# Linear attention between two mixture-of-experts halves on one core: the attention of each sequence in other visits, and later gathers for phase 2

## The reference

```python
x = x + 0.5 * ffn(layernorm(x), W1, b1, W2, b2, Wg, bg)      # first half: "f = 0"
x = x + attn(layernorm(x), Wq, Wk, Wv, proj)
x = x + 0.5 * ffn(layernorm(x), W1, b1, W2, b2, Wg, bg)      # second half: "f = 1"

def ffn(x):    # x is 2 x 2048 x 128; 4 experts, 128 -> 512 -> 128
    idx = argmax(softmax(x @ Wg + bg))                       # one expert per token
    y_e = gelu(x @ W1[e] + b1[e]) @ W2[e] + b2[e]
    return y_e for e = idx
def attn(x):   # linear attention, 32 features
    q', k' = elu(q @ proj) + 1, elu(k @ proj) + 1
    kv = sum over the sequence of k' (outer) v
    return (q' @ kv) / (sum(q') + 1e-8)
```

## Time and profile before

| what | value |
|---|---|
| median of 3 runs | 236.23 us (235.95 to 236.77) |
| the profiled execution's own time | 237.53 us |
| its span, first to last instruction | 235.8 us |
| mean granted clock of TensorE | 0.969 |
| busy: PE, DVE, ACT, POOL | 207.2, 159.4, 126.9, 160.2 us |
| last `finish` on DVE ends | 224.8 us |
| last scatter on POOL ends | 234.2 us |

### The profile page before, as it was taken

How to read it: one execution, slowest core, us unless ns; L and a number is a source line. 1 busy time by engine, 2 the same in 40 slices (tenths; PEclk the granted TensorE clock), 3 DMA queues, 4 the chain that set the end, 5 groups by cost and what they waited for, 6 DMA issues and landing times. The chain is left out here.

```text
span 235.8 us, 6375 instructions
## 1 busy us (share of the span) xinstructions
PE 207.2 (88%) x1786; PEld 195.7 (83%) x1786; DVE 159.4 (68%) x641; ACT 126.9 (54%) x406; POOL 160.2 (68%) x225
## 2 busy tenths in 40 slices
PE   8989996996997999999969998999959899999900
PEld 7879996896997988889969897779959899999900
DVE  3699463579688989698887879788776545553400
ACT  1415055567554586635675676825565567765500
POOL 7221888882728687147138888756878888788775
PEclk9999999998899999999999999999979999999985
DMA  4999259982534462326703852517721976662111
GB/s 103 372 321 254 96 199 351 314 212 83 185 110 167 154 215 69 130 106 237 277 0 116 300 206 83 165 61 281 269 79 42 329 274 222 222 221 103 45 56 45
DMA packets 28454, 41.69 MB, mean 177 GB/s; under 512 B 7795, under 2 KB 14851, under 8 KB 28422
## 3 DMA queue, kind: packets, MB, share of 16 engines
q1 hardware_dynamic: 22368, 34.11, 40.5%
q0 software_dynamic: 3072, 6.82, 11.1%
q10 hardware_dynamic: 2982, 0.36, 1.0%
HBM read 9.41 MB, written 6.82 MB: 69 GB/s over the span
## 5 line engine op out<-in xcount | busy, mean ns | idle before, releaser
L1145 ACT ACTIVATE hT<-U,slab 128x128 f32<-128x128 f32 x304 | 86.7, 370 | 56.4 <-PE U L966 56.3
L966 PE MATMUL U<-hT_in,slab 128*128 (+1 forms) x608 | 82.8, 280 | 1.5 <-ACT hT_in L1139 1.3
L977 PE MATMUL DN<-W,hT 128*128 (+1 forms) x608 | 83.7, 282 | 0.2 <-issue 0.2
L966 PEld LDWEIGHTS U<-hT_in,slab 128*128 128x128 f32 x608 | 74.8, 194 | 2.7 <-issue 2.4
L977 PEld LDWEIGHTS DN<-W,hT 128*128 128x128 f32 x608 | 75.4, 195 | 1.4 <-issue 1.2
L430 POOL DMA_INDIRECT G<-rows,src x64 | 62.5, 977 | 15.2 <-issue 10.2
L729 DVE SCALAR_TENSOR_TENSOR G<-DN,mask,G 128x128 f32 (+1 forms) x76 | 26.4, 348 | 27.3 <-PE DN L977 24.6
L416 POOL MEMSET rest<- 128x512 f32 (+1 forms) x78 | 35.4, 454 | 6.3 <-DVE G L729 0.7
L442 POOL DMA_INDIRECT out_dram<-G x32 | 31.6, 988 | 7.3 <-issue 6.3
L705 DVE TENSOR_SCALAR xn<-G 128x128 f32<-128x128 f32 x64 | 23.7, 389 | 9.3 <-DMA G<-rows,src 9.0
L717 DVE SCALAR_TENSOR_TENSOR G<-slab,mask,G 128x128 f32 (+1 forms) x60 | 21.2, 353 | 6.7 <-DVE G L729 4.0
(11 more groups left out here) (159 smaller groups left out, 219.7 us busy)
## 6 DMA issues: line engine op xcount, KB each, us to landing
slab<-W SPq DMA_DIRECT2D x76, 322.0 KB, 3.1
rows<-G SPq DMA_DIRECT2D x8, 288.0 KB, 2.1
rows<-X SPq DMA_DIRECT2D x4, 512.0 KB, 9.5
X<-in_L_attn_x_dram SPq DMA_DIRECT2D x4, 256.0 KB, 6.7
X<-in_L_attn_x_dram SPq DMA_DIRECT2D x2, 512.0 KB, 8.8
W<-in_L_ffn_W_dram SPq DMA_DIRECT2D x1, 1024.0 KB, 11.5
W<-in_L_ffn_W_dram SPq DMA_DIRECT2D x4, 256.0 KB, 6.0
G<-rows,src POOLq DMA_INDIRECT x64, 3.2
```

Of the source, the lines that this page charges most:

```text
L966: i = eng.matmul(U[s % 3][:, c * P:(c + 1) * P], slab[s % NSLAB][:, c * P:(c + 1) * P], hT_in[ph % 2][:, bass.ds(v * P - expert_at[s], P)] ...
L977: i = eng.matmul(DN[s % 2][:, 0:D], hT[s % NHT][:, c * P:(c + 1) * P], W2[:, bass.ds(expert_at[s] + c * NE * D, D)], start=(c == 0 and not ...
L1145: i = eng.activation(hT[s % NHT][:, c * P:(c + 1) * P], U[s % 3][:, c * P:(c + 1) * P], ACT.Gelu, bias=slab[s % NSLAB][:, F + c:F + c + 1])
```

## The change

It does five things.
1. Attention: group 3's `side_turn` goes ahead of `down` in visit 0, and its `side_kq`, `la_scaled` and exponential follow in the same visit. All four exponentials stand together in visit 0 (one load of a table there, one back in visit 1), where three stood at the end of the phase before and one in visit 1. `la_features` takes groups 0, 1 and then 2, 3. `la_z` is one division over all 16 tiles. `la_fold` moves to visit 2, and the four `lb_num` to visits 3, 4, 4, 5 (before 4, 4, 5, 6), with the `lb_x2` in visits 3, 4, 4, 5.
2. The norms of tiles 8 to 11 stand together in visit 3, those of tiles 12 and 13 (phase 1) or 12 to 15 (phase 2) in visit 5.
3. HOT1 is 6 and no longer 7, and `counts` and `inverse` stand ahead of `up` in their visits and no longer behind it. In phase 2 `inverse` stays in visit 10, where it was.
4. `route_slots` no longer makes the two small tables `end_i` and `flo_i`; `visit_tables` makes them.
5. POOL: the gathers of phase 2 begin in visit LATE1 = 12 (before 11), with ten of them before phase 2 and six in its visits 0 to 2 (before twelve and four). The gathers of phase 3 begin in visit FIRST1 = 10 (before 11). Six scatters stand ahead of them (before seven), and 26 follow (before 25).

The diff, cut to its core:

```diff
-        NORM_MID = (-5, -4, -3, -2, -1, 0, 0, 1, 1, 2, 2, 3, 4, 5, 7, 8)
-        NORM_EARLY = (-5, -4, -3, -2, -1, 0, 0, 1, 1, 2, 2, 3, 4, 5, 6, 6)
+        NORM_MID = (-5, -4, -3, -2, -1, 0, 0, 0, 3, 3, 3, 3, 5, 5, 7, 8)
+        NORM_EARLY = (-5, -4, -3, -2, -1, 0, 0, 0, 3, 3, 3, 3, 5, 5, 5, 5)
-        HOT0, HOT1 = 5, 7
-        FIRST0, FIRST1 = HOT0 + 4, HOT1 + 4
+        HOT0, HOT1 = 5, 6
+        FIRST0, FIRST1, LATE1 = HOT0 + 4, HOT1 + 4, 12
@@ gpsimd
-                if ph > 0 and v == 4:
-                    pow_lb(o, 0)
-                if ph == 2 and v == 4:
-                    scatter(0, 0)
-                if ph > 0 and 4 <= v < 3 + NG:
-                    pow_lb(o, v - 3)
+                if ph > 0 and v in (4, 5, 6):
+                    pow_lb(o, v - 4)
+                if ph > 0 and v == 6:
+                    pow_lb(o, 3)
-            EARLY0, NEXT0, NEXT1 = 8, V - FIRST0, 3 * (V - FIRST1) // 2
-            SCATTERS = {5: (1,), 6: (2,), 7: (3,), 8: (4,), 9: (5,), 10: (6,)}
-            DONE0, PAIRS1 = 7, 10
+            EARLY0, NEXT0, NEXT1 = 8, V - FIRST0, 3 * (V - LATE1) // 2
+            SCATTERS = {v: (v - 4,) for v in range(4, FIRST1)}
+            DONE0, PAIRS1 = FIRST1 - 4, 10
@@ phase 1
-                if v not in (FIRST1, FIRST1 + 1):
-                    attention_pow(1, v)
+                attention_pow(1, v)
-                if v >= FIRST1:
-                    gather_first(1, 0, s, v - FIRST1)
-                if v in (FIRST1, FIRST1 + 1):
-                    attention_pow(1, v)
+                if v >= LATE1:
+                    gather_first(1, 0, s, v - LATE1)
@@ phase 2
-                if v + NEXT1 < T:
-                    gather(1, 0, v + NEXT1)
+                for t in range(NEXT1 + 2 * v, min(NEXT1 + 2 * v + 2, T)):
+                    gather(1, 0, t)
@@ vector, route_slots
-                did(eng.tensor_copy(end_i[:, :], c3[:, 0:NE - 1, T - 1]))
-                did(eng.tensor_scalar(flo_i[:, :], end_i[:, :], 7, None, ALU.arith_shift_right))
@@ vector, by visit (o = ph - 1)
+                if ph in (1, 2) and v == 3:
+                    la_kv(o)
                 finish(s)
                     if v == 1:
-                        la_scaled(o, NG - 1)
+                        la_features(o, 2, NG)
+                        la_z(o, 0, NG)
                     if v == 2:
-                        la_features(o, NG - 1, NG)
-                        la_z(o, NG - 1, NG)
-                    if v == 3:
                         la_gt(o)
-                        la_kv(o)
                     if v == 4:
-                        lb_x2(o, 0)
                         lb_x2(o, 1)
-                    if v in (5, 6):
-                        lb_x2(o, v - 3)
+                        lb_x2(o, 2)
+                    if v == 5:
+                        lb_x2(o, 3)
...
+                if ph in (1, 2) and v == 0:
+                    la_scaled(o, NG - 1)
...
-                        la_features(o, 0, NG - 1)
-                    if v == 1:
-                        la_z(o, 0, NG - 1)
+                        la_features(o, 0, 2)
+                    if v == 3:
+                        lb_x2(o, 0)
@@ tensor, ahead of up
+                if ph < B + 1 and v == hot_at + 2:
                     counts(ph + 1)
+                if ph in (1, 2) and v == hot_at + 4:
+                    inverse(ph + 1, 0, NG)
@@ scalar
-                if late and v == 1:
-                    la_exp(ph - 1, 3, 4)
+                    if v == 0:
+                        la_exp(o, 0, NG)
-                if ph < B and v == 18:
-                    la_exp(ph, 0, 3)
```

More of the change, by code:

```diff
@@ L641, in route_slots @@
                 need(eng, rt["cb"], ph)
-                did(eng.tensor_tensor(wh3[:, :, :], wh[:, :, :], hot[:, :, :], ALU.mult), False)
-                did(eng.tensor_copy(end_i[:, :], c3[:, 0:NE - 1, T - 1]))
-                did(eng.tensor_reduce(pos[:, :], te(wh3), AX.X, ALU.add), False)
-                did(eng.tensor_scalar(flo_i[:, :], end_i[:, :], 7, None, ALU.arith_shift_right))
+                did(eng.tensor_tensor(wh3[:, :, :], wh[:, :, :], hot[:, :, :], ALU.mult))
+                did(eng.tensor_reduce(pos[:, :], te(wh3), AX.X, ALU.add))
                 did(eng.tensor_copy(pos_i[:, :], pos[:, :]))
@@ L661, in visit_tables @@
                 e_no = exp_no[:, 1:NE, 0]
+                ends = cum[:, :].rearrange("p (e t) -> p e t", e=NE)[:, 0:NE - 1, T - 1]
+                did(eng.tensor_copy(end_i[:, :], ends))
+                did(eng.tensor_scalar(flo_i[:, :], end_i[:, :], 7, None, ALU.arith_shift_right))
                 did(eng.scalar_tensor_tensor(out=vis[:, :], in0=flo_i[:, :], scalar=float(T - 1), in1=e_no, op0=ALU.min,
@@ L1018, in la_q @@
             def la_q(b):
-                need(eng, la["z"], 2 * b + 1)
+                need(eng, la["z"], b)
                 for g in range(NG):
@@ L1074, in _ @@
                 ph, v = divmod(s, V)
+                hot_at = HOT0 if ph == 0 else HOT1
+                o = ph - 1
+                if ph in (1, 2) and v == 0:
+                    side_turn(o, NG - 1)
                 down(s)
+                if ph in (1, 2):
+                    if v == 3:
+                        la_kv(o)
+                        la_q(o)
+                    if v == 4:
+                        lb_num(o, 1)
+                    if v == 5:
+                        lb_num(o, 3)
                 for ahead in groups_of(ph, v):
                     turn_in(*ahead)
-                hot_at = HOT0 if ph == 0 else HOT1
                 if ph in (1, 2):
-                    o = ph - 1
                     if v == 0:
-                        side_turn(o, NG - 1)
-                    if v == 1:
                         side_kq(o, NG - 1)
-                    if v == 3:
-                        la_q(o)
-                        la_fold(o)
-                    if v in (4, 5, 6):
-                        lb_num(o, (0, 2, 3)[v - 4])
-                if ph == 0 and v == hot_at + 2:
+                    if v == 2:
+                        la_sum(o, 2, 4)
+                if ph < B + 1 and v == hot_at + 2:
                     counts(ph + 1)
+                if ph in (1, 2) and v == hot_at + 4:
+                    inverse(ph + 1, 0, NG)
                 if ph == 0 and v == hot_at + 4:
@@ L1105, in _ @@
                     if v == 2:
-                        la_sum(o, 2, 4)
-                    if v == 3:
-                        la_kv(o)
-                    if v == 4:
-                        lb_num(o, 1)
-                    if v == hot_at + 2:
-                        counts(ph + 1)
-                    if v == hot_at + (3 if ph == 2 else 4):
-                        inverse(ph + 1, 0, NG)
+                        la_fold(o)
+                    if v in (3, 4):
+                        lb_num(o, 2 * (v - 3))
                 if ph == 0 and v == hot_at + 3:
@@ L1206, in _ @@
                 ph, v = divmod(s, V)
+                if ph in (1, 2) and v == 0:
+                    side_copy((ph - 1) * NG + NG - 1)
                 for ahead in groups_of(ph, v):
```

13 lines of the change are left out of this document (6 added, 7 removed).

## The result

The changed kernel takes 238.22 us (median of 8 runs, 237.07 to 240.03), the kernel before beside it 236.24 us (median of 8, 235.27 to 237.21): ratio 1.0083, 95% interval 1.0054 to 1.0112. It is 2 us slower. The forecast was 234.1 us and faster, with a range up to 237.2. The profiled execution took 238.72 us, with a span of 237.0.

What follows compares the result with a forecast made beforehand. POOL's last unbroken run of gathers and scatters bounds the end, not PE. Its start 3.5 us sooner, less 1.4 for one more scatter, gives -2.1: 235.4 profiled, 1.3 less for the median, 234.1 us; range 232.3 to 237.2.

Steps and rivals of the forecast that it cites:

- The gathers of phase 2: POOL, end of phase 1: first gather issued at 126.0, 2.8 us later than before, behind two powers.
- rival B: DVE, visits 11 and 12 of phase 1: group 1's variance later than about 126, so slower, 236.6 us; chance 0.17.
- signs of being wrong: Final run's start not moving, POOL waiting in it, or group 3's power before 140 or after 144.
- the start of the final run: POOL's phase 3 gathers, then scatters, without waits: start at 172.8, or 3.5 us sooner than 176.05 with phase 0's gain.
- the power of group 3: POOL, phase 2: 9 gathers and one power, 16.1 us after the first gather, so 142.1, no sooner than before.
- the gain of phase 1: Attention and routing of phase 1: counts at 110.5 against 114.27, bounded by 1.0 and 3.8 us earlier.
- PE's wait for the first norm of phase 2: PE, start of phase 2: 2 to 3 us ahead, it waits for the first gather, landing at 129.2.
- rival A: Attention of phase 2: PE's clock falls behind new waits, 1.5 of 3.5 us left, 236.1 us, same time; chance 0.2.
- The tail: POOL, end of the kernel: one more scatter is left for it, costing 1.36 us.
- The slow cast of `end_i`: DVE, `route_slots`: removing it gains 0.15 to 0.55 us per routing; `pos_i` might meet the memset instead.
- Rival C: Group 1's variance sooner or fewer gathers ahead of group 3's power, 1.5 us sooner: 232.6 us; chance 0.13.
- the 0.3 of phase 0: Routing of phase 0: two steps leave `route_slots`, so everything after is 0.3 us earlier, added at the end.

Runs made afterwards that it cites:

- e5: The kernel before, unchanged, run again to have a second profile of it: 236.46 us, ratio 1.0019.
- e6: The changed kernel, unchanged, run again: 238.42 us, ratio 1.0091 to the kernel before.
- e7: Changed kernel with phase 2's gathers begun in visit 11 and group 1's power behind the gathers of visit 12: 234.35 us, ratio 0.9912 to the kernel before.
- e2: Changed kernel with the gather of visit 12 ahead of group 1's power, gathers still from visit 12: 252.91 us, 1.0089, on the chip where all were slow.
- e8: e7 with phase 1's visit tables and masks one visit later, behind group 1's variance: 232.99 us, ratio 0.9847 to the kernel before.
- e12: e8 with seven scatters of phase 2 ahead of phase 3's gathers and 25 behind: 233.61 us, ratio 0.987 to the kernel before.
- e9: Kernel before with only phase 2's gathers begun in visit 12, behind group 1's power, six of them in phase 2: 236.98 us, ratio 1.0037.
- e4: Same kernel as e9, run on the chip where all were slow: 251.82 us, ratio 1.0028 to the kernel before.

## Why the prediction was wrong

**The step that failed is "The gathers of phase 2", in its term for the variance of group 1** (124.0 forecast, 126.06 measured). The mechanism was right, its size was not. The chain was added up as if DVE did only the steps named:
- variance of group 0: 118.1 forecast, 119.14 measured. 0.7 of it lies between the counts and A's end in phase 1, 2.83 instead of 2.1, with a `finish`, a norm and a row's statistics in between; the rest is 0.3 up to `src` and 0.2 behind it, less 0.1 for the counts;
- from there to the end of `la_scaled`: 1.9 forecast, 2.67 measured, since a `finish` that waits 0.75 for PE, a residual and a row's statistics stand ahead of it (120.99 instead of the power's end at 120.32);
- tables and masks: 2.45 forecast, 2.38 measured;
- `finish`, residual and aggregate: 1.5 forecast, 1.87 measured, with 0.64 of it a wait.

That makes 2.1, and the variance crosses the 126 which rival B named. What came true is rival B: its place, and slower, though 1.6 us more than its 236.6. But not by its reason: the routing of phase 1 did come at the forecast 110.5 (110.36). Two of the prediction's own signs of being wrong came: the start of the final run hardly moved (0.3), and the power of group 3 came after 144.

**That 110.36 met 110.5 was luck in part.** The terms given for the gain of phase 1 (1.8, 0.9 and 0.6) make 3.3, and the prediction took 3.8, the end of its own bounds. Like for like it is 2.6 (112.82 in e5, 110.24 in e6). The rest of the 3.9 between the two traces is in the main the 1.45 by which the profile of before was late.

**What hung on it.** The first gather was 1.9 late (126.0 forecast), the power of group 3 2.0 (142.1 forecast), and the times between them were right: 16.1 forecast, 16.2 measured. PE's wait for the first norm of phase 2 came as forecast, at 131.46 instead of 129.2, and 3.31 long. In e7 it isn't there: it is a sign of the late gathers. Whether it costs anything by itself no run separates; up to the power of group 3 it doesn't, for in e6 the clock was 0.50 behind it and the power came at 144.00, in the changed kernel's first profile 1.00 and 144.09.

**The terms that held.** From the power's start to kv's end 9.5 forecast, 9.7 measured; kv to `lgn` 12.1 and 12.4; `lgn` to the counts 2.8 and 2.6; counts to A's end 2.3 and 2.4; no clock lost at `la_sum` (rival A): behind PE's wait of 1.75 the granted clock was 1.00. Rival A is no idle fear, though: e2 shows it, see above. The tail: 1.36 forecast, 35.44 less 34.0 measured, 1.44. The slow cast of `end_i` is gone from `route_slots`, and `pos_i` met no memset (0.17 at 170.19), so from the counts to A's end it takes 2.40 where it took 3.17. A cast can still meet a memset in another execution, see below. Rival C's "DVE idles 1.7" was read in a stretch of phase 2 (12.35 less 10.63) and says nothing of the variance in phase 1, which came later than forecast and not sooner.

**The start of the final run: 172.5 forecast (with the 0.3 of phase 0), 175.77 measured.** 2.4 of it is A, late with all the rest (171.19 for 168.8). The other 0.9 is a term left out: behind `AV`, which waits for A, stand two more scatters with their memsets, so the run can't start earlier than A's end plus 4.6 us, and `src`, ready at 174.71, is not what it waits for. The prediction counted the pieces of POOL's queue as one sum with 1.5 of waits, and did not ask which of them are behind the last wait.

**An error of method, 1.3 us.** The forecast 110.5 already left that lateness of 1.45 behind. The profiled execution's distance of 1.3 to the median is, as far as the two profiles show, the same loss (e5's profiled execution took 236.07, 1.46 less than 237.53), and it was taken off the forecast once more at the end. Final run 3.3, tail 0.1, method 1.3, and 0.5 that the profile after lies above its median, subtracted: 4.2, for 238.2 less 234.1.

**What paid.** The reordered attention and routing do: with the old order of POOL they make the kernel 0.9% faster (e7), and with the tables behind the variance 1.5% (e8, 232.99 us), the fastest version, which beats both kernels. e12, with 0.987, can't be told from it.

## What to carry to other kernels

A queue that is full to its end turns a wait at its head into time at its end, as far as nothing behind it has room to spare (from e7 to e6 the power of group 3 is 3.5 us later and the last scatter 3.7, from e5 to e9 2.0 and 0.9): before an instruction that waits is put ahead of a run of others, add up what its producer's engine does before it, the waits of the pieces in between included, and compare with how long the run behind it has been ready (here 10.4 us). Look for stretches of low granted clock in the profile of before ahead of counting any gain against it, and don't correct for the same loss twice. At the start of the final run ask which item of the queue waits last, and count from there.

## What the runs showed of the hardware

*The clock after a gap of PE differs between executions of one kernel.* Ahead of the stretch from 58 us PE waited 1.91 us in one profile of before and 1.69 in the other; the granted clock then was 0.50 and 1.00. In phase 2 both have a gap of 2.2 us ahead of the inverse, and the clock behind it (174 to 176) was 0.50 in the first and 1.00 in the other. Near 40 us it is the other way round: 1.00 from 42 to 44 behind a gap of 2.25, and 0.50 behind one of 2.03. The changed kernel waits 3.3 us for the first norm of phase 2 in both of its profiles, and from 132 to 134 the clock was 1.00 in one and 0.50 in the other (e6).

*A small cast or `tensor_scalar` of DVE on an SBUF operand that meets a memset of POOL ends no sooner than it.* Timeline of POOL and DVE of the changed kernel, at one such place:

```profile
140.69 0.53 POOL L416 MEMSET rest<- 128x512 f32 x1
140.78 0.46 DVE L737 TENSOR_SCALAR VE<-MV 128x4 f32<-128x4 f32 x1
```

Both end near 141.23. In e5 the cast of `end_i` takes 0.56, from 167.83 to 168.39, the memset ends at 168.37; in e9 0.32, from 168.91 to 169.23, the memset at 169.21; alone it takes 0.16. This bears out what the Trainium skill says (SBUF — State Buffer, Who interferes with whom): the loser waits out the whole instruction. Which of the two loses these records don't tell: in e5 the cast's begins 0.02 ahead of the memset's. A `tensor_reduce` is not held up: in the trace of before one of 0.26 at 50.67 lies inside a memset from 50.64 to 51.16. Such a cast took between 0.16 and 0.57 in these traces, by the accident of its start.

*All kernels of a round can be some 14 us slower.* In round 1 the kernel before had a median of 250.18 us over 35 runs, in round 3, on the chip with the same number, 236.57 over 29. Up to the final run nothing differed: e4 and e9 are one kernel, and its final run's first gather stands at 176.23 and 176.16.
